# A transformer block with eight experts: the first batch's tokens scattered into slots by expert

## The chip, the cores and the metric

The kernel runs on one core of a Trainium2 chip. A core has a matrix engine (TensorE, PE in the profile, with its weight loads as PEld), VectorE (DVE), ScalarE (ACT), GpSimd (POOL) and a sync engine (SP), each with an instruction queue of its own; semaphores order them. The metric is the device time of one execution in microseconds, lower is better. Before the change it is 930.87 us, the median of three runs (930.03 to 931.92).

## What is computed

One block on x of 2 batches x 1024 tokens x 256 features, in float32. Cut to what matters:

```python
mod = (silu(c) @ wmod).reshape(2, 6, 1, -1)
sa, ca, ga, sb, cb, gb = mod[:, 0], ..., mod[:, 5]
ga = (2 * (ga >= 0) - 1) * maximum(abs(ga), 0.25)       # gb likewise
h = layernorm(x) * (1 + ca) + sa
# 16 query heads of 128 over 4 key heads, sinusoidal positions, causal softmax, projection by wo
x = x + ga * attention(h)
h = layernorm(x) * (1 + cb) + sb
logits = h @ gate_w.T                                   # 8 experts
top_vals, top_idx = top_k(logits, 2)
w = softmax(top_vals)
y_all = einsum('td,eod->teo', h, expert_w) + expert_b   # 256 -> 256 for each expert
x = x + gb * sum(y_all[top_idx] * w)
```

The reference computes all eight experts for every token and picks two; only the two chosen outputs matter.

## The kernel before

Every float32 product is made from a high and a low part of each operand, in three matrix products (high x high, high x low, low x high: `moving_late` L594, `held_late` L602). So each operand is cut on its way: ScalarE writes the high part (`keep_hi`, L1008), VectorE or GpSimd subtracts it for the low part.

The work is two batches of 16 heads ("frames"), then an expert stage. `n` counts the heads of both batches, `l` those of one. Frames 1 to 12 of a batch stand in a loop of three rounds of four, the others are written out. A frame has 12 steps `q` (`STEPS`): in each, TensorE turns a block of probabilities into bank `ps_t` (`turn_probs`, L713), computes a piece of the next head's scores (`ps_s`, L604 to L608), weighs values (`ps_o`, L596 to L600, L723), and, at given steps, the queries of the next head (`queries`, into `ps_m`) and the projection of the previous one by wo (`project`). VectorE masks (L1346), finds the row maximum (L1352), makes low parts of the turned probabilities (`pt_lo`, L1361), brings queries with their bias and position to `raw` (L1378), takes the reciprocal of the row sums (L1390) and adds projections to `acc` (L1399). ScalarE does the exponential (L1058) and the high parts. GpSimd cuts wq and wo of coming heads (L462 to L476) and makes `q_lo` (L483); its order in a frame is q_lo of the next head's second half, cut wq, cut wo, q_lo of the head after it. The sync queue (SP) loads wq and wo head by head (L342, L346).

The scale and shift vectors of the first LayerNorm's modulation and of the second's are computed at the start as columns (`modulate`, L626, 16 products each, read by VectorE); the two gate vectors `ga` and `gb` are needed as rows, and are computed near the end of the heads: one `modulation_rows` (L767) for each batch in heads 14 and 15 of the second batch, from `repeat_silu` and with four VectorE operations (`modulation_part`). In the last head TensorE also turns the expert weights (`turn_weights`), which ScalarE and VectorE cut into `we_hi`, `we_lo`, and the first hidden tile is turned and gated.

The expert stage then runs densely over 16 tiles of 128 tokens, both batches alike. For a tile TensorE does `experts` (four groups, 24 products of 512 columns in all), `turn_coef`, `turn_hidden` (L776) and `gate` (L785) of the next tile, and `mix_bias`. VectorE picks the two best experts (`choose`, from L1589, with the coefficients to L1605), and sums the eight outputs with the token's coefficients (`mix`, eight operations on 128x256), with `statistics` (L1520) and `normalise` of later tiles. GpSimd does `residual` (all of the first batch ahead), `inverse_deviation`, `hidden_lo` and `finish` (three operations, L543 to L550), and SP stores the tile.

The order on every engine is the order of the program; waits stand in front of the instruction that needs them. A wait therefore holds up everything behind it on its engine.

## Time and profile before

| | us |
|---|---|
| Median of three runs | 930.87 (930.03 to 931.92) |
| The profiled execution | 930.91 |
| Span of its trace | 929.1 |
| TensorE busy | 903.3 (97%) |
| VectorE busy | 784.0 (84%) |
| ScalarE busy | 535.6 (58%) |
| GpSimd busy | 274.5 (30%) |

The span reaches from the first to the last recorded instruction; the 1.8 us between it and the execution's time lie outside the trace. A busy share is an average over stages with different limits, so the stages are read one by one, in windows. All times of trace rows are in microseconds from the start of the span, unless they say ns. A row of a timeline or of the chain gives start, length, engine, line and operation, its output and inputs with their shapes and, in brackets, how long the engine had been idle and what released it. "x4" merges four instructions. In the windows "PEclk" is the granted clock of TensorE as a share of 2.4 GHz and "DMA" the mean busy share of the 16 DMA engines. A "q" behind an engine's name (PEldq, SPq) is its queue, which handles registers and DMA issues.

### The profile page before, as it was taken

What the parts mean: (1) busy time and instruction counts of PE and PEld (TensorE: products, weight loads), DVE (VectorE), ACT (ScalarE), POOL (GpSimd) and SP (SyncE); (2) the same over time, 40 slices, a digit from 0 to 9 for tenths busy, and PEclk for the clock granted to TensorE, in tenths of its full rate; (3) what the DMA queues carried; (4) which work ended last, traced back from release to release, by engine and by line L of the source; (5) the groups of instructions that cost most, each with busy time, mean ns of one, the idle gap of its engine ahead of it and who ended that gap; (6) DMA issues with size and microseconds to landing.
All of it is one profiled execution on the core that took longest, in us unless ns stands there. A gap on an engine that the chain in (4) does not pass through costs nothing.

```text
span 929.1 us, 18211 instructions
## 1 busy us (share of the span) xinstructions
PE 903.3 (97%) x5353; PEld 782.5 (84%) x5353; DVE 784.0 (84%) x1775; ACT 535.6 (58%) x1224; POOL 274.5 (30%) x346
## 2 busy tenths in 40 slices
PE   5999999999999999999999999999999999999997
PEld 4688889888898888978888888998888889767775
DVE  5777888888888888888888888888888888899996
ACT  4587666666666666655666666666666655422231
POOL 3454222222222222123322222222222212466544
PEclk9999999999999999999999999999999999999999
DMA  6000000000000000100000000000000022100000
GB/s 215 7 12 13 12 13 12 12 17 17 11 11 11 11 11 7 57 6 1 24 12 12 14 12 11 11 11 11 11 11 11 12 74 92 46 12 17 23 17 24
DMA packets 23764, 21.60 MB, mean 23 GB/s; under 512 B 1530, under 2 KB 22564, under 8 KB 23716
## 3 DMA queue, kind: packets, MB, share of 16 engines
q1 hardware_dynamic: 23652, 20.99, 7.2%
q8 instruction: 24, 0.39, 0.2%
q14 instruction: 24, 0.20, 0.1%
q10 hardware_dynamic: 64, 0.02, 0.0%
HBM read 18.91 MB, written 2.10 MB: 23 GB/s over the span
## 4 chain that ended last, share of the span: by engine, by line
PE 87%; DVE 8%; issue 2%; ACT 1%; DMA 1%; POOL 0%; DVEq 0%; SPq 0%; POOLq 0%; ACTq 0%
PE ps_t L713 13%; PE ps_s L604 9%; PE ps_s L608 9%; PE ps_s L605 9%; PE ps_o L596 7%; PE ps_o L600 7%; PE ps_o L597 6%; PE ps_m L604 3%; PE ps_m L608 3%; PE ps_m L605 3%; PE ps_m L596 3%; PE ps_m L600 3%; PE ps_m L597 3%; PE ps_o L723 1%; DVE acc L1399 1%
## 5 line engine op out<-in xcount | busy, mean ns | idle before, releaser
L1008 ACT ACTIVATE pt_hi<-ps_t 128x512 fp32r<-128x512 f32 (+2 forms) x320 | 170.8, 534 | 142.9 <-PE ps_t L713 142.8
L1058 ACT ACTIVATE probs<-ps_s,neg_max 128x128 f32<-128x128 f32 (+7 forms) x256 | 189.8, 742 | 78.5 <-DVE neg_max L1352 76.5
L1361 DVE TENSOR_TENSOR pt_lo<-ps_t,pt_hi 128x512 fp32r<-128x512 f32 (+2 forms) x320 | 192.3, 601 | 12.7 <-ACT pt_hi L1008 7.6
L1352 DVE TENSOR_REDUCE neg_max<-ps_s 128x1 f32<-128x128 f32 (+7 forms) x256 | 192.6, 752 | 3.7
L713 PE MATMUL ps_t<-ident,probs 128*128 128x128 f32 x1152 | 188.4, 272 | 2.1 <-DVE pt_lo L1361 2.1
L483 POOL TENSOR_TENSOR q_lo<-raw,q_hi 128x512 fp32r<-128x512 f32 x60 | 77.4, 1290 | 358.5 <-ACT q_hi L1008 358.5
L713 PEld LDWEIGHTS ps_t<-ident,probs 128*128 128x128 f32 x1152 | 141.5, 140 | 26.0 <-DVE pt_lo L1361 8.2
L604 PE MATMUL ps_s<-k_hi,q_hi 128*128 128x512 f32 (+2 forms) x354 | 148.6, 420 | 2.3 <-ACT probs L1058 2.3
L1399 DVE SCALAR_TENSOR_TENSOR acc<-ps_m,rsum,acc 128x256 f32<-128x256 f32 x256 | 111.5, 477 | 24.0 <-PE ps_m L608 24.0
L1346 DVE TENSOR_TENSOR ps_s<-ps_s,mask 128x128 f32<-128x128 f32 x256 | 75.7, 296 | 56.6 <-PE ps_s L608 49.8
L608 PE MATMUL ps_s<-k_hi,q_lo 128*128 128x512 f32 (+2 forms) x354 | 123.4, 349 | 0.0
L605 PE MATMUL ps_s<-k_lo,q_hi 128*128 128x512 f32 (+2 forms) x354 | 122.5, 346 | 0.0
L596 PE MATMUL ps_o<-pt_hi,v_hi 128*128 128x512 f32 (+2 forms) x320 | 119.8, 374 | 0.7 <-DVE o_lo L1366 0.7
L600 PE MATMUL ps_o<-pt_lo,v_hi 128*128 128x512 f32 (+2 forms) x320 | 115.6, 361 | 0.0
L597 PE MATMUL ps_o<-pt_hi,v_lo 128*128 128x512 f32 (+2 forms) x320 | 115.1, 360 | 0.0
L604 PEld LDWEIGHTS ps_s<-k_hi,q_hi 128*128 128x128 f32 x354 | 66.9, 189 | 8.0 <-issue 3.2
L604 PE MATMUL ps_m<-wo_hi,o_hi 128*128 128x256 f32 x256 | 72.7, 284 | 0.4 <-DVE acc L1399 0.3
L608 PE MATMUL ps_m<-wo_hi,o_lo 128*128 128x256 f32 x256 | 72.2, 282 | 0.0
L608 PEld LDWEIGHTS ps_s<-k_hi,q_lo 128*128 128x128 f32 x354 | 66.4, 188 | 6.8
L605 PE MATMUL ps_m<-wo_lo,o_hi 128*128 128x256 f32 x256 | 72.1, 282 | 0.0
L605 PEld LDWEIGHTS ps_s<-k_lo,q_hi 128*128 128x128 f32 x354 | 67.6, 191 | 1.9
L600 PEld LDWEIGHTS ps_o<-pt_lo,v_hi 128*128 128x128 f32 x320 | 60.1, 188 | 8.4
(180 smaller groups left out, 1718.3 us busy)
## 6 DMA issues: line engine op xcount, KB each, us to landing
wq_raw<-in_L_attn_wq_dram SPq DMA_DIRECT2D x32, 128.0 KB, 2.2
wo_raw<-in_L_attn_wo_dram SPq DMA_DIRECT2D x32, 128.0 KB, 2.1
wkv_raw<-in_L_attn_wkv_dram SPq DMA_DIRECT2D x2, 1024.0 KB, 6.9
we_raw<-in_L_ffn_expert_w_dram SPq DMA_DIRECT2D x1, 2048.0 KB, 12.1
x_again<-in_L_attn_x_dram SPq DMA_DIRECT2D x2, 1024.0 KB, 10.0
out_dram<-y_out SPq DMA_DIRECT2D x16, 128.0 KB, 1.7
acc<-in_L_attn_x_dram SPq DMA_DIRECT2D x2, 512.0 KB, 4.1
wmod_sb<-in_L_wmod_dram SPq DMA_DIRECT2D x2, 512.0 KB, 8.4
```

The lines of the kernel that those rows point to most:

```text
L596: nc.tensor.matmul(out_ap, a[0], b[0], start=start, stop=False)
L597: nc.tensor.matmul(out_ap, a[1], b[0], start=False, stop=False)
L600: return nc.tensor.matmul(out_ap, a[0], b[1], start=False, stop=stop)
L604: nc.tensor.matmul(out_ap, a[0], b[0], start=start, stop=False)
L605: nc.tensor.matmul(out_ap, a[0], b[1], start=False, stop=False)
L608: return nc.tensor.matmul(out_ap, a[1], b[0], start=False, stop=stop)
L713: last = pe.transpose(ps_t[:, q % 2, col:col + P], probs[par][:, p0:p0 + P], ident[:, :])
L1008: return nc.scalar.activation(dst, src, ACT.Copy, scale=scale)
L1058: nc.scalar.activation(probs[par][:, prob_offset(i):prob_offset(i) + w], ps_s[:, i % 2, col:col + w], ACT.Exp, bias=neg_max[:, par, i:i + ...
L1352: nc.vector.tensor_reduce(neg_max[:, par, i:i + 1], ps_s[:, i % 2, col:col + w], AXIS_X, ALU.max, negate=True).then_inc(max_set, 1)
L1361: nc.vector.tensor_tensor(pt_lo[:, q % PT, lo:CH], ps_t[:, q % 2, lo:CH], pt_hi[:, q % PT, lo:CH].bitcast(F32), ALU.subtract).then_inc(pt_ ...
L1399: last = nc.vector.scalar_tensor_tensor(row, ps_m[:, i * E:(i + 1) * E], rsum[:, par, tile:tile + 1], row, ALU.mult, ALU.add)
```

## The change

The first batch (1024 tokens, eight tiles) no longer goes through the dense stage. The second batch does, as before.

- *Modulation.* All six vectors are now computed as columns at the start: a third `modulate` of 16 products, with `gate_columns` (four VectorE operations) for `ga` and `gb`. GpSimd spreads columns over 128 columns (`spread_columns`), TensorE turns them into rows in side steps, and ScalarE copies them out (`side_read`). `modulation_rows`, `repeat_silu` and `modulation_part` go.
- *The first batch's rows.* During heads 1 to 8 of the second batch GpSimd does the residual and the modulated LayerNorm of one tile a head (`first_residual`, two operations; `hidden_row`, a power and three operations of 128x256), VectorE its statistics (`row_statistics`, three operations). TensorE turns the tile at step 3 and gates it at step 10 of heads 2 to 9 (`side_step`), ScalarE reads both.
- *Placing.* In head 10 VectorE finds each token's two experts and weights and counts them, 33 small operations (`choose_first`); at step 3 of head 12 TensorE ranks tokens with two products (`rank`); in the same head VectorE makes every token's two places and the 23 slots' experts, 15 operations (`place_rows`).
- *Scattering.* In heads 13 and 14 GpSimd writes the rows to `slot_rows_dram` by eight indirect DMAs each, between wo's cut and the next q_lo. Each expert's tokens fill whole slots of 128 rows; 23 slots hold any distribution (2048 choices / 128 + 7). The buffer is filled with x before, so that rows that no token takes are finite.
- *The slot stage* stands ahead of the dense one: SP loads 20 + 3 slots after the last scatter and the last head's scores; each is turned, cut and multiplied by the one expert of the slot (six products of 256 columns), which TensorE picks by a register; VectorE adds the bias row of that expert, by a register as well, and SP stores the slot to `slot_out_dram`. Turn and gate of the second batch's first four tiles stand between the slots.
- *Collecting.* In the dense stage, now eight tiles, GpSimd gathers each first-batch token's two output rows by indirect DMA (two for each tile, four in each of the first four steps), ScalarE weighs one, VectorE weighs the other, adds, applies the gate and adds the residual (`join`, three operations), and SP stores.
- The second batch's heads are written out in full in place of the loop, since their work now differs from head to head.

The core of the diff:

```diff
+SLOTS = 2 * T // P + EXPERTS - 1
+SLOT_PLANES = 3
+SLOT_OUT = 3
+HELD_SLOTS = 20
+AHEAD = 4
...
+SIDE = ([("rows", 0, q, v) for q, v in ((2, 0), (3, 1), (10, 2), (11, 3))]
+        + [u for i in range(NT) for u in (("turn", 2 + i, 3, i), ("gate", 2 + i, 10, i))]
+        + [("rank", 12, 3, 0)]
+        + [("rows", HEADS - 1, q, v) for q, v in ((2, 0), (3, 1))])
+SIDE_AT = {(l, q): (s, kind, i) for s, (kind, l, q, i) in enumerate(SIDE)}
...
+            sp.wait_ge(scattered, 16 * FREE * NT)
+            sp.dma_start(x_again[1][:, :, :], x_tiles[:, NT:2 * NT, :]).then_inc(x_again_in[1], 16)
+            sp.wait_ge(t_mm, NS * (B * HEADS - 1))
+            sp.wait_ge(s_mm, NT * B * HEADS)
+            sp.wait_ge(q_lo_set, NC * B * HEADS)
+            slot_v = slot_dram.rearrange("(s p) e -> p s e", p=P)
+            half = HELD_SLOTS // 2
+            sp.dma_start(slot_rows[:, 0:half, :], slot_v[:, 0:half, :]).then_inc(slots_in[0], 16)
+            sp.dma_start(slot_rows[:, half:HELD_SLOTS, :], slot_v[:, half:HELD_SLOTS, :]).then_inc(slots_in[1], 16)
+            sp.dma_start(slot_rows_more[:, :, :], slot_v[:, HELD_SLOTS:SLOTS, :]).then_inc(slots_in[2], 16)
+            sp.dma_start(ebias_all[:, :, :].rearrange("p x o -> p (x o)"),
+                         expert_b.rearrange("x o -> (x o)").partition_broadcast(P)).then_inc(ebias_in, 16)
...
+                sp.wait_ge(slot_out, s + 1)
+                sp.dma_start(y_dram[s * P:(s + 1) * P, :], y_slot[:, s % SLOT_OUT, :]).then_inc(y_stored[s % SLOT_OUT], 16)
...
+            def scatter_rows(i):
+                if i == 0:
+                    pool.wait_ge(place_set, 1)
+                    pool.wait_ge(row_set, NT)
+                    pool.wait_ge(slots_filled, 32)
+                for f in range(FREE):
+                    pool.indirect_dma_start(
+                        slot_dram, bass.IndirectOffsetOnAxis(ap=r_place_u[:, f, i:i + 1], axis=0),
+                        x_rows[:, i, :], None).then_inc(scattered, 16)
...
+            def gather(i):
+                if i == 0:
+                    for j in range(SLOT_OUT):
+                        pool.wait_ge(y_stored[j], 16 * len(range(j, SLOTS, SLOT_OUT)))
+                for f in range(FREE):
+                    pool.indirect_dma_start(
+                        picked[:, f, i, :], None, y_dram,
...
+            for m in range(NT):
+                for i in (2 * m, 2 * m + 1):
+                    if i < NT:
+                        gather(i)
+                if m + 6 < NT:
+                    normalise(m + 6)
+                if m > 0:
+                    finish(m - 1)
+                if m + 2 < NT:
...
-            def modulation_rows(b, bank):
-                pe.wait_ge(silu_b_set, 1)
-                pe.wait_ge(gmod_in, 48)
-                for m in range(2):
+            def side_step(l, q):
+                s, kind, i = SIDE_AT[l, q]
+                spare = ps_t[:, q % 2, :]
+                if kind == "rows":
+                    spread = spread0 if l == 0 else spread1
+                    pe.wait_ge(spread_set, KE * (i + 1) + (0 if l == 0 else 4 * KE))
                     for k in range(KE):
+                        last = pe.transpose(spare[:, k * P:(k + 1) * P], spread[:, i * KE + k, :], ident[:, :])
+                elif kind == "turn":
+                    pe.wait_ge(row_set, i + 1)
+                    for k in range(KE):
+                        last = pe.transpose(spare[:, k * P:(k + 1) * P], x_rows[:, i, k * P:(k + 1) * P], ident[:, :])
+                elif kind == "gate":
+                    pe.wait_ge(side_set, side_count("turn", i))
+                    for k in range(KE):
+                        last = pe.matmul(spare[:, 0:EXPERTS], row_t[:, k, :], gate_t[:, k, :],
...
+            def slot_product(s, e):
+                if s == 0:
+                    pe.wait_ge(we_lo_set, EXPERTS // 2 * KE)
+                if s >= 2:
+                    pe.wait_ge(slot_out, s - 1)
+                pe.wait_ge(slot_hi_set, s + 1)
+                for k in range(KE):
+                    w = [t[:, k, bass.ds(e, 1), :].rearrange("p x o -> p (x o)") for t in (we_hi, we_lo)]
+                    i = s % SLOT_PLANES
+                    last = held_late(kv_bank(2 + s % 2)[:, 0:O], (slot_hi[i][:, k, :], slot_lo[i][:, k, :]), w,
+                                     k == 0, k == KE - 1, (slot_lo_set, s + 1) if k == 0 else None)
+                last.then_inc(slot_mm, 1)
...
+            _, slot_e = nc.values_load_multi_w_load_instructions(
+                slot_expert_u[0:1, 0:SLOTS], engines=[mybir.EngineType.PE], min_val=0, max_val=EXPERTS - 1,
+                skip_runtime_bounds_check_because="a sum of seven comparisons lies in 0 to 7")
+            for s in range(SLOTS):
+                if s + 2 < SLOTS:
+                    turn_slot(s + 2)
+                slot_product(s, slot_e[s])
...
+            def choose_first(q):
...
+                    nc.vector.tensor_tensor(r_weight[:, 1, :], r_egap[:, :], r_weight[:, 0, :], ALU.mult)
+                    nc.vector.memset(r_before[:, 0, :], 0.0)
+                    nc.vector.tensor_copy(r_before[:, 1, :], r_both[:, 0, :]).then_inc(r_dve, 1)
+                    for i in range(1, NT):
+                        dve.wait_ge(r_dve, done + 6 + i)
+                        nc.vector.tensor_tensor(r_before[:, i + 1, :], r_before[:, i, :], r_both[:, i, :],
+                                                ALU.add).then_inc(*((r_dve, 1) if i + 1 < NT else (r_count_set, 1)))
...
+            def slot_finish(s, e):
+                dve.wait_ge(slot_mm, s + 1)
+                if s == 0:
+                    dve.wait_ge(ebias_in, 32)
+                if s >= SLOT_OUT:
+                    dve.wait_ge(y_stored[s % SLOT_OUT], 16 * (s // SLOT_OUT))
+                nc.vector.tensor_tensor(y_slot[:, s % SLOT_OUT, :], kv_bank(2 + s % 2)[:, 0:O],
+                                        ebias_all[:, bass.ds(e, 1), :].rearrange("p x o -> p (x o)"),
+                                        ALU.add).then_inc(slot_out, 1)
...
+            def join(i):
+                par = i % 2
+                dve.wait_ge(first_part_set, i + 1)
+                nc.vector.scalar_tensor_tensor(both_parts[:, par, :], picked[:, 1, i, :], r_weight[:, 1, i:i + 1],
+                                               first_part[:, par, :], ALU.mult, ALU.add).then_inc(join_step, 1)
+                dve.wait_ge(join_step, 2 * i + 1)
+                nc.vector.tensor_tensor(both_parts[:, par, :], both_parts[:, par, :], mod_rows0[:, 1, :],
+                                        ALU.mult).then_inc(join_step, 1)
+                if i >= 2:
+                    dve.wait_ge(joined_done[par], 16 * (i // 2))
+                dve.wait_ge(join_step, 2 * i + 2)
+                nc.vector.tensor_tensor(joined[:, par, :], both_parts[:, par, :], acc[:, i, :],
+                                        ALU.add).then_inc(joined_set, 1)
```

## Rows read from the trace of the kernel before

**Rows 1.** Windows: length, busy us: PE, PEld, DVE, ACT, POOL; PEclk, DMA, GB/s.
```profile
0.00:23.00 23.00, 13.18 (x51) 11.31 (x52) 13.65 (x43) 10.37 (x17) 8.85 (x18) 1.00 0.62 218
474.00:770.00 296.00, 295.04 (x1865) 264.37 (x1864) 254.53 (x532) 186.40 (x422) 61.65 (x76) 1.00 0.07 21
804.30:923.50 119.20, 116.58 (x536) 86.63 (x534) 106.14 (x364) 34.71 (x109) 62.32 (x91) 1.00 0.05 17
891.60:912.90 21.30, 21.30 (x101) 16.15 (x100) 18.56 (x64) 6.65 (x22) 9.70 (x14) 1.00 0.06 20
923.50:929.10 5.60, 0.00 (x0) 0.00 (x0) 0.87 (x2) 0.00 (x0) 2.17 (x3) 0.80 0.07 23
```

**Rows 2.** Waits of the looped heads, 474 to 770: us, times, longest.
```profile
PEld ps_t L713 <- DVE pt_lo L1361: 2.6, 13, 0.2
```

**Rows 3.** Timeline, VectorE: one rsum reciprocal ends each head.
```profile
570.92 0.17 DVE L1390 RECIPROCAL rsum<-sums 128x4 f32<-128x4 f32 x1
...
593.30 0.17 DVE L1390 RECIPROCAL rsum<-sums 128x4 f32<-128x4 f32 x1
...
749.90 0.17 DVE L1390 RECIPROCAL rsum<-sums 128x4 f32<-128x4 f32 x1
...
773.64 0.17 DVE L1390 RECIPROCAL rsum<-sums 128x4 f32<-128x4 f32 x1
```

**Rows 4.** Chain of waits: start, length, engine, work.
```profile
776.64 1.73 PE ps_m L767 x8
...
808.78 0.12 PE ps_m L605
...
809.38 0.23 PE ps_t L776 x2
...
885.15 0.54 PE ps_o L785 x4
...
886.72 0.23 PE ps_s L605
```

**Rows 5.** Line 998, a register instruction on TensorE's queue (least/median/largest ns).
```profile
L998 PEldq FUSED_REGOPS  x3: 50/55/55, 811.6 to 871.3; - x3
```

**Rows 6.** Timeline, VectorE: a pt_lo of 128x256.
```profile
575.01 0.39 DVE L1361 TENSOR_TENSOR pt_lo<-ps_t,pt_hi 128x256 fp32r<-128x256 f32 x1
```

**Rows 7.** Groups by line and form, 790 to 929: busy us, mean ns, idle.
```profile
L1520 DVE BATCH_NORM_STATS2 st<-acc 128x6 f32 x12 | 5.0, 418 | 0.0
...
L1605 DVE TENSOR_TENSOR wtop<-egap,wtop 128x1 f32<-128x1 f32 x16 | 4.2, 260 | 0.5
```

**Rows 8.** Timeline: a VectorE CAST alone, then one beside GpSimd's finish.
```profile
866.51 0.17 DVE L1599 CAST top_f<-top_i 128x2 f32<-128x2 uint32 x1
...
887.11 0.75 POOL L550 TENSOR_TENSOR y_out<-y_sum,acc 128x256 f32<-128x256 f32 x1 [0.28 <-POOL y_sum L547]
887.12 0.76 DVE L1599 CAST top_f<-top_i 128x2 f32<-128x2 uint32 x1
```

**Rows 9.** Line 342, issues of the sync queue (ns).
```profile
L342 SPq DMA_DIRECT2D wq_raw<-in_L_attn_wq_dram x30: 368/373/1283, 60.6 to 726.5; - x30
```

**Rows 10.** Page, section 6: DMA issues.
```profile
wq_raw<-in_L_attn_wq_dram SPq DMA_DIRECT2D x32, 128.0 KB, 2.2
...
we_raw<-in_L_ffn_expert_w_dram SPq DMA_DIRECT2D x1, 2048.0 KB, 12.1
```

**Rows 11.** Timeline: one head's first turns, and GpSimd's wo_hi and q_lo.
```profile
555.69 0.60 PE L713 MATMUL ps_t<-ident,probs 128*128 128x128 f32 x4
...
567.84 0.40 POOL L473 TENSOR_SCALAR wo_hi<-wo_raw 128x256 fp32r<-128x256 f32 x1 [4.83 <-PE ps_m L608]
...
577.93 1.28 POOL L483 TENSOR_TENSOR q_lo<-raw,q_hi 128x512 fp32r<-128x512 f32 x1 [8.87 <-ACT q_hi L1008]
```

**Rows 12.** Timeline, TensorE at the start: a modulation, a wait for raw.
```profile
28.43 1.95 PE L626 MATMUL ps_m<-silu_c,wmod_sb 128*128 128x2 f32 x16 [0.15 <-DVE v_bias L1552]
...
44.08 0.50 PE L604 MATMUL ps_t<-wv_hi,h_hi 128*128 128x512 f32 x1 [1.30 <-DVE raw L1322]
```

966 lines of the change are left out of this document (601 added, 365 removed).

## The prediction

> **What bounds the kernel now.** I read the table of windows first: in the looped heads of batch 1 TensorE is busy 295.0 of 296 us [rows 1]. The list of waits says that this is a true bound: over the same stretch its only repeated wait is for pt_lo, 2.6 us in 13 pieces [rows 2]. One head takes 22.38 us, from one rsum reciprocal to the same of the next head [rows 3]. So whatever the change puts on TensorE inside the heads comes out in full; VectorE has 14% of each head free, some 3.1 us (254.5 of 296 us busy [rows 1]), ScalarE and GpSimd much more. Then the windows: the dense expert stage runs from 804.3 to 923.5, 119.2 us for 16 token tiles [rows 1], 7.45 us a tile. From 891.6 to 912.9 TensorE is busy all of 21.3 us for three tiles, 7.1 us each [rows 1]; the chain of waits gives 0.23 us for a 512-column product and 0.12 for a 256-column one [rows 4], so 24 products of 512 columns are 5.5 us of a tile. The last 5.6 us are GpSimd's finish and the store, with the clock falling only there [rows 1].
>
> **What the change takes away: half of the dense stage.** Batch 0's eight tiles (24 products of 512 columns each) go, and 23 slots come, each with two transposes (0.23) and six products of 256 columns (6 x 0.12): 0.95 us of TensorE [rows 4], 21.9 in all against 8 x 5.5 = 44. That is the core gain, 22 us; the slots are counted for the worst case, so the columns fall to 1 part in 2.8 and not to a quarter. In the slot stage stand also what batch 1 needs ahead: four turns (0.23) and gates (0.54), 3.1 us, and two projections, 1.4. A slot's weights are picked by a register: per product perhaps one register instruction, which costs 0.050 to 0.055 us on TensorE's queue [rows 5], 6 a slot; hidden they cost nothing, bare 7 us over the stage.
> VectorE in the slot stage: two 128x256 operations a slot (0.39 each [rows 6]), 18 us, six statistics at 0.9 (0.42 and two short ones [rows 7]), four best-two choices at 0.7, three coefficient chains at 1.1 to 2.2 and four accumulations (1.7): 32 us. Both engines near 30 us, with two-deep banks between them, so they don't overlap fully: bounds 28 us (TensorE alone, with 1.6 us of first latency) and 42 (bare register work, and half of VectorE's 13 us of extra pieces uncovered). I take 37, nearer the upper, since each slot's transposes wait for the VectorE operation two slots back. Batch 1's dense tiles: four at 7.1, then four without turn and gate (0.23 + 0.54 [rows 4]) at 6.33, 53.7; the second tile is VectorE's (mix 3.3, eight at 0.39 and what lies between, statistics 0.9, choice and coefficients 2.3, the new join's three operations 1.3: 7.8), another 0.9. With 0.5 between the stages: 37 + 0.5 + 54.6 = 92.1.
>
> **GpSimd in the dense stage.** It now issues two indexed gathers for each of eight tiles, four in each of the first four steps, ahead of its old work there (finish 3 x 0.73 [rows 8], hidden_lo 0.73, normalise 1.0). No row shows a transfer issued by GpSimd. Bounds for one issue, g: 0.37 us, which an issue on the sync queue holds its queue for [rows 9], and 2.1, as if GpSimd were held until a 128 KB transfer lands (2.2 from issue to landing [rows 10]). I take 1.5, nearer the upper, because 128 row numbers are read and turned into addresses by program, and a 128x256 pass of GpSimd alone is 0.73. GpSimd begins about 3 us late (the last slot store must be issued and land, about 2.2). Step 0: 3 + 4g + 1.7 = 10.7; step 1: + 4g + 1.0 + 0.73 = 18.5 until tile 0's sum is out, which tile 2's mix waits for at 15.5 us: 3 late; steps 2 and 3 are each 4g + 2.9 = 8.9 against 7.1: 1.8 and 1.9 late. Sum 7 us; at g = 1.0 it is nothing, at 2.1 it is 16.
> The Trainium skill, DMA: Bandwidth & Descriptors, Specifications, gives a first byte after about 1 us for a GpSimd transfer and 0.6 for a sync one; taken as g = 1.0 this would strike the 7 us. No run here shows either.
>
> **What it adds in the heads.** TensorE, all at full price: 12 turns at 0.23 (four of the modulation rows, eight of hidden rows), eight gates at 0.54, one ranking product of two fp32 pieces at about 0.6 (bounds 0.24, two at a 256-column product's 0.12, and 1.7, a modulation product's group): 7.7 us [rows 4]. VectorE: row_statistics, 0.9 in eight heads, is under the 3.1 us of slack, nothing (4 us if it weren't). Head 10's choice is 33 small operations at about 0.22 (260 ns is the mean of such a one [rows 7], 0.17 the least [rows 8]), 7.3 us in one head that has 3.1 free, a third of which lies after the work: 3.5 us late, bounds 0 (spread over the next head) and 6. Head 12's placing, 15 at 0.26, 3.9: 1.0 late. GpSimd: residual and hidden row, 4.2 us a head, lie in its long waits (8.87 us before one q_lo [rows 11]); nothing. Its scatters, eight in head 13 and eight in head 14, stand behind wo's cut and in front of the next q_lo. The cut starts 12.15 us into the head and ends at 13.4; the scatters take 8g = 12, q_lo 1.3: ready at 26.7, wanted by the next head's second score piece, 3.2 us into it, at 25.6 (the head begins at its first turns, 555.69 [rows 11]): 1.1 us. The unrolled second batch adds fetches but no wait that I can see: heads 13 and 14 of batch 0, outside its loop, take the same 22.4.
> Start: a third modulation, 16 products in 1.95 us [rows 12], and gate_columns, four VectorE operations (1.0 at 0.26 each), lie ahead of the first queries, with some 0.9 from engine to engine between them. TensorE is 3.9 late, and it later gives back the waits for raw (1.3 us in one piece [rows 12], some 0.5 in smaller ones): 2.0 (bounds 1 and 4). The spread columns lie in GpSimd's idle head; nothing.
>
> **Heads 14 and 15.** The two products for modulation rows go: head 14 was 23.74 against 22.38 [rows 3], so 1.4 back. In head 15 go the 1.73 us product [rows 4], one turn and gate (0.8), and VectorE loses some 8 us of modulation and statistics, with which 2 us of TensorE's waits go; two row turns and two slot turns come (0.9): 3.6 back.
> But the sync queue waits for all scatters before it loads the slots: they end 13.4 + 8g = 25.4 into head 14 and land 2 later, 5 us into head 15. Then 4.9 MB follow (x 1.0, slots 2.9, the bias rows 1.0). we_raw's 2 MB landed in 12.1 with about 1.5 MB beside it [rows 10], some 270 GB/s: 18 us, so the bias rows, last in line, land about 24 us into head 15. TensorE is through at 19.6, then both engines load 23 expert numbers into registers (unseen; 23 times 0.05, a register instruction, or 0.26, a small VectorE operation: 1 to 6 us, I take 2), and slot 0's finish wants the bias at 22.9. Registers and bias together: 4 us (bounds 1 and 14).
>
> **The sum.** Start 2.0, TensorE in heads 7.7, choice and placing 4.5, q_lo 1.1, heads 14 and 15 -5.0, registers and loads 4.0, expert stages 92.1 + 7 - 119.1 = -20.0: together -5.7 against the span of 929.1. 923.4, and with the 1.8 us that lie outside it in the profiled execution (930.9, which is the median too) 925.2 us.
>
> **Rivals.** (A) *GpSimd keeps up.* With g at 1.0 or less the 7 us and the 1.1 go, 2 of the loads' 4, and with cheap registers the slots take 32: 925.2 - 15.1 = 910. For it: GpSimd is idle 48% of the dense stage now [rows 1].
> (B) *Slower: GpSimd becomes the bound*, at scatters and gathers both. It decides from g of about 1.7: by the same steps the dense stage then loses 9.8 in place of 7, q_lo and the slot loads 1.6 more each, 6.0 together, and the gain is gone. At 2.1: 9 + 4.8 + 4.8, and 3 in the slots, 947. For it: an operation on VectorE that took 0.17 alone takes 0.76 beside GpSimd's pass [rows 8], so these two hold each other up, and the dense stage has both busy. The Trainium skill, SBUF — State Buffer, A bandwidth-pool intuition that's wrong, tells of a GpSimd transfer of 0.62 us that took 3.1 beside a VectorE copy, since its descriptors couldn't be written; a g of 3.1 would by the steps above give some 980, an estimate. Nothing here shows it, and most VectorE operations in these stages read PSUM.
> (C) *The clock falls in the slot stage*, where small products stand between waits: if a third of its 27 us of TensorE work ran at 1.2 GHz, +8: 933. Against: in the first 23 us TensorE is busy 57% and is granted 2.4 GHz; lower levels appear only after its last product [rows 1].
> That the change doesn't do what it says I give nothing: fixed counts make the work the same whatever the routing.
>
> **Chances.** The sum 45% (its own range 917 to 934: faster 0.33, same 0.05, slower 0.07), A 26%, B 23%, C 6% (slower, but for 0.01). Within 0.2% (1.9 us, about what a measurement can tell) 0.07; faster 0.59; slower 0.34. The low end takes the slots at 32 us, no wait for GpSimd and a choice half hidden (905); the high end is B with little more (949).
>
> **What would show it.** TensorE's heads 2 to 9 of batch 1 at 23.1 us, head 10 near 26; in head 13 a wait for q_lo; the scatters' and gathers' own spans on GpSimd near 1.5; slot stage 37, dense stage 61 to 62 with mixes waiting for y_sum; ebias as the last releaser of slot 0. Wrong it would be if an indexed issue is far from 1.5, if register-addressed products take longer than 0.12 by more than 0.05, or if the long VectorE heads are absorbed.

## The result

The changed kernel takes 915.37 us, the median of four runs (914.43 to 916.02), against 931.28 of the kernel before (the median of four as well); the ratio is 0.983, its 95% interval 0.9813 to 0.9847. Its profiled execution has a span of 913.8 us, 15.3 less than before. The forecast was 925.2 in a range of 905 to 949: the right side, and the time inside the range, but a gain of 6 us where 16 were measured. The step that failed is the sum of the stages behind the heads: it had the slots at 37.5 us with the piece between the stages, where the trace has 32.7, and GpSimd's gathers at 7 us on top of the dense stage, where it has 2.6.

Busy time on the page of the profile after (before: TensorE 903.3, VectorE 784.0, GpSimd 274.5):

```profile
PE 877.7 (96%) x5337; PEld 768.4 (84%) x5337; DVE 758.9 (83%) x1725; ACT 531.9 (58%) x1223; POOL 320.9 (35%) x395
```

The windows of the changed kernel, to be read against [rows 1] (length, busy time of PE, PEld, DVE, ACT, POOL, then clock, DMA share, GB/s). They are a stretch of the second batch's heads, TensorE's wait ahead of the slots, the slot stage, the dense stage and the tail:

```profile
470.00:760.00 290.00, 289.41 (x1849) 259.72 (x1848) 255.89 (x591) 182.06 (x427) 102.90 (x133) 1.00 0.04 13
814.75:816.15 1.40, 0.01 (x2) 0.03 (x1) 0.66 (x2) 0.60 (x1) 0.00 (x0) 1.00 0.02 6
816.15:848.86 32.71, 29.20 (x216) 25.58 (x217) 27.14 (x100) 12.80 (x38) 20.62 (x26) 1.00 0.25 82
848.86:906.10 57.24, 55.62 (x242) 39.91 (x240) 47.08 (x142) 14.99 (x47) 39.97 (x47) 1.00 0.23 71
906.10:913.80 7.70, 0.13 (x1) 0.00 (x0) 4.57 (x8) 0.00 (x0) 2.40 (x3) 0.85 0.21 69
```

TensorE is still busy all through the heads (289.4 of 290 us). The slot stage is 32.7 us, the dense stage of eight tiles 57.2 with 55.6 of TensorE, and the tail 7.7 against 5.6 before. The heads' lengths, from one rsum reciprocal to the next as in [rows 3] (the second of each head; the first pair spans head 3, the last three rows heads 14 and 15):

```profile
511.60 0.17 DVE L1674 RECIPROCAL rsum<-sums 128x4 f32<-128x4 f32 x1
...
534.53 0.17 DVE L1674 RECIPROCAL rsum<-sums 128x4 f32<-128x4 f32 x1
...
763.75 0.17 DVE L1674 RECIPROCAL rsum<-sums 128x4 f32<-128x4 f32 x1
...
787.79 0.17 DVE L1674 RECIPROCAL rsum<-sums 128x4 f32<-128x4 f32 x1
...
811.76 0.17 DVE L1674 RECIPROCAL rsum<-sums 128x4 f32<-128x4 f32 x1
```

A head that holds a turn and a gate takes 22.93 us against 22.38, head 14 is 24.04 and head 15 23.97. Put together against the trace before, in us:

| | forecast | measured |
|---|---|---|
| start, to the last head of batch 0 | +2.0 | +3.2 |
| turns, gates, rows and ranking on TensorE | +7.7 | +4.7, ranking in the next row |
| choice, ranking and placing (heads 10 to 13) | +4.5 | +1.9 |
| what goes from heads 14 and 15 | -5.0 | -6.0 |
| scatters' harm to heads 14 and 15 | +1.1 | +5.8 |
| between the heads and slot 1's products | +4.0 | +2.1 |
| slots | 37 + 0.5 | 32.7 |
| dense stage | 54.6 + 7 | 57.2 |
| tail | 5.6 | 7.7 |

TensorE is through with the heads 10.45 us later than before (814.75 against 804.3; the first five rows give 9.6, and 0.8 of the sixth lies ahead of that moment), and the expert stages with the tail are 99.05 us against 124.8: together -15.3. The row of heads 14 and 15 is split with the first experiment, which has them without scatters: 22.40 and 19.79, against 23.74 and 24.41 before. So the forecast had the moment at which the heads end nearly right (+10.3), by errors that cancel, which is luck, and the whole miss of 9.6 us lies behind it.

The row of the start holds something that isn't work. In this profiled execution the granted clock fell for a while at the start, which it didn't before the change. The same stretch in the changed kernel and in the paced run below, whose start is the same:

```profile
24.00:40.00 16.00, 14.08 (x68) 11.05 (x67) 9.77 (x30) 8.44 (x17) 7.67 (x7) 0.89 0.04 10
...
24.00:40.00 16.00, 14.27 (x77) 11.43 (x76) 10.90 (x31) 8.50 (x18) 7.30 (x7) 1.00 0.03 10
```

From the second modulation to TensorE's first wait for a row of probabilities it is 36.8 us in the first and 35.2 in the second (27.69 to 62.89): the lower clock cost 1.6 us, and it comes in some executions and not in others.

What harmed heads 14 and 15 is seen in the timeline of ScalarE and TensorE (the bracket gives the idle time before and what ended it), and in two windows:

```profile
769.56 0.60 ACT L1233 ACTIVATE pt_hi<-ps_t 128x512 fp32r<-128x512 f32 x1 [2.89 <-remote]
...
771.40 0.35 PE L787 MATMUL ps_s<-k_hi,q_hi 128*128 128x256 f32 x1 [1.39 <-ACT probs L1283]
...
793.39 0.60 ACT L1233 ACTIVATE pt_hi<-ps_t 128x512 fp32r<-128x512 f32 x1 [4.22 <-remote]
...
794.77 0.44 PE L954 MATMUL ps_t<-ident,spread 128*128 128x128 f32 x2 [3.70 <-DVE pt_lo L1645]
...
790.00:794.00 4.00, 1.07 (x10) 0.83 (x8) 1.38 (x2) 0.61 (x2) 3.07 (x6) 1.00 0.27 98
794.00:800.00 6.00, 5.23 (x27) 4.77 (x28) 3.44 (x7) 3.54 (x9) 0.00 (x0) 0.72 0.88 280
```

ScalarE stood 2.9 us ahead of head 14's first pt_hi and 4.2 ahead of head 15's, "remote" being a releaser that the profile can't name; both came free 1.4 us after the end of the last scatter of a row of eight. TensorE lost 1.4 and 3.7 us. After the second its granted clock fell to the lower of its two levels for a while: 0.72 is the mean of 794 to 800, a mixture of 1.2 and 2.4 GHz. The scatters themselves (shortest, median and longest ns):

```profile
L642 POOL DMA_INDIRECT slot_rows_dram<-x_again,r_place_u x16: 956/960/1263, 758.0 to 791.0; - x16
```

0.96 us each, and 0.30 between two: g is 1.26 us.

### The profile page after: what moved, and what is told of

Same layout as the page of the kernel before. It is cut to its first block, busy times and chain, and to the rows that moved or that the text cites. A ratio compares the mean times of both kernels' runs of the same rounds, so it can differ in the third digit from the quotient of the medians.

```text
span 913.8 us, 16758 instructions
## 1 busy us (share of the span) xinstructions
PE 877.7 (96%) x5337; PEld 768.4 (84%) x5337; DVE 758.9 (83%) x1725; ACT 531.9 (58%) x1223; POOL 320.9 (35%) x395
## 4 chain that ended last, share of the span: by engine, by line
PE 84%; DVE 7%; POOL 2%; issue 2%; ACT 2%; DMA 1%; another core or an unknown queue 0%; SPq 0%; DVEq 0%; ACTq 0%; POOLq 0%
PE ps_t L898 13%; PE ps_s L787 8%; PE ps_s L791 8%; PE ps_s L788 8%; PE ps_o L783 7%; PE ps_o L779 7%; PE ps_o L780 7%; PE ps_m L787 3%; PE ps_m L791 3%; PE ps_m L788 3%; PE ps_m L779 3%; PE ps_m L783 3%; PE ps_m L780 3%; PE ps_o L908 1%; POOL picked L737 1%
```

## Experiments

All times that follow are medians, with the ratio to the kernel before on the same chip; the changed kernel itself stands at 0.983.

### No scatters

```diff
-                    pool.indirect_dma_start(
-                        slot_dram, bass.IndirectOffsetOnAxis(ap=r_place_u[:, f, i:i + 1], axis=0),
-                        x_rows[:, i, :], None).then_inc(scattered, 16)
+                    pool.sem_inc(scattered, 16)
```

> Leaves the 16 scatters out (the slots then hold rows of x, so the output isn't the reference's); GpSimd raises the semaphore itself, so everything that waits for them goes on. Theory 1: the scatters' transfers are what ScalarE waits for at the starts of heads 14 and 15 (2.9 and 4.2 us, TensorE 1.4 and 3.7 us behind it, then 1.6 us lost at 1.2 GHz). Then all of it goes, head 14 comes to about 22.5 us and head 15 to 20, and the kernel takes about 908.5. Rival: those waits belong to the heads written out in full, whose instructions have to be fetched, and stay without scatters: then no more than 1 us is gained, 914.5.

909.28 us, ratio 0.9769 (0.9747 to 0.9791). ScalarE isn't held, TensorE doesn't wait, and the reciprocals of heads 14 and 15 (that of head 13 was at 763.12) show heads of 22.40 and 19.79 us:

```profile
785.52 0.17 DVE L1672 RECIPROCAL rsum<-sums 128x4 f32<-128x4 f32 x1
...
805.31 0.17 DVE L1672 RECIPROCAL rsum<-sums 128x4 f32<-128x4 f32 x1
```

Theory 1 holds: 5.8 us of the two heads are the scatters' doing, and the heads' code being written out isn't enough for it: it is as long here, but for the 16 scatters.

### Plain transfers in place of the scatters

```diff
-                    pool.indirect_dma_start(
-                        slot_dram, bass.IndirectOffsetOnAxis(ap=r_place_u[:, f, i:i + 1], axis=0),
-                        x_rows[:, i, :], None).then_inc(scattered, 16)
+                    pool.dma_start(slot_dram[(f * NT + i) * P:(f * NT + i + 1) * P, :],
+                                   x_rows[:, i, :]).then_inc(scattered, 16)
```

> Each scatter is replaced, at its place, by a plain GpSimd transfer of the same 128 rows to fixed places (the rows are then not sorted by expert, so the output isn't the reference's). Theory A: it is the indexed form that holds ScalarE (TensorE waits 1.4 and 3.7 us); then both waits vanish, heads 14 and 15 take 22.4 and 19.8, about 909. Theory B: any GpSimd transfer at that place does it; then the waits stay, 915. An issue is expected at 0.4 to 1.3 us.

911.37 us, ratio 0.9792 (0.9776 to 0.9808). Heads 14 and 15 take 22.40 and 19.79 again: theory A, it is the indexed form. The issues of that line (shortest, median and longest ns):

```profile
L642 POOL DMA_DIRECT2D slot_rows_dram<-x_again x16: 542/542/808, 759.6 to 785.7; - x16
```

0.54 us for a plain transfer of 128 KB on GpSimd, against 1.26 for an indexed one.

### The scatters elsewhere in their heads, in groups of four, and paced

```diff
+                if b == 1 and l == SCATTER_FRAMES[1]:
+                    for i in range(4, NT):
+                        scatter_rows(i)
                 if nxt2:
                     cut_wq(n + 2, par)
+                if b == 1 and l == SCATTER_FRAMES[0]:
+                    scatter_rows(0)
+                    scatter_rows(1)
```

(Tiles 2 and 3 stay behind wo's cut in head 13.)

> The same 16 scatters, earlier in their heads: in head 13 four after wq's cut and four after wo's, in head 14 all eight right after the first q_lo, so that none is under way when a head ends. Theory: ScalarE is held only where scatters fall on the few instructions at a head's end (766 to 769 and 789 to 793 us); moved away, heads 14 and 15 take 22.4 and 19.8 as without scatters, 909.5. Rival 1: ScalarE is held wherever eight scatters run, the waits only move: 915. Rival 2: GpSimd's late wo cut (by some 4 us in head 14) becomes a wait of TensorE: 912.

912.66 us, ratio 0.9817 (0.9801 to 0.9833). Behind head 13's two groups of four nobody waits long. In head 14 the eight in a row, now from 771.5 to 781.3, hold ScalarE there:

```profile
777.22 0.60 ACT L1238 ACTIVATE o_hi<-ps_o 128x512 fp32r<-128x512 f32 x1 [1.88 <-remote]
778.66 0.60 ACT L1238 ACTIVATE pt_hi<-ps_t 128x512 fp32r<-128x512 f32 x1 [0.84 <-remote]
...
782.26 0.88 DVE L1688 SCALAR_TENSOR_TENSOR acc<-ps_m,rsum,acc 128x256 f32<-128x256 f32 x2 [2.28 <-remote]
...
783.06 1.09 ACT L1238 ACTIVATE pt_hi<-ps_t 128x512 fp32r<-128x512 f32 x2 [2.86 <-remote]
```

Head 14 takes 26.22 us and head 15 18.91. So ScalarE is held at either place of the row of eight, which is rival 1 for head 14, and it isn't held alone: VectorE, too, stood 2.3 us without a releaser that the profile can name. The groups of four left head 13 at 21.46 us, against 21.40 in the changed kernel.

From that kernel, the row of eight is split in two:

```diff
                 if b == 1 and l == SCATTER_FRAMES[1]:
-                    for i in range(4, NT):
-                        scatter_rows(i)
+                    scatter_rows(4)
+                    scatter_rows(5)
...
-                if b == 1 and l == SCATTER_FRAMES[0]:
-                    scatter_rows(2)
-                    scatter_rows(3)
+                if b == 1 and l in SCATTER_FRAMES:
+                    k = 2 + 4 * SCATTER_FRAMES.index(l)
+                    scatter_rows(k)
+                    scatter_rows(k + 1)
```

> The 16 scatters in four groups of four: in head 13 after wq's and after wo's cut, in head 14 after the first q_lo and after wo's cut. In the run with head 13's groups of four and head 14's eight together, ScalarE was held in head 14 only. Theory: a row of eight is what holds it, four are taken without a wait: head 14 about 22.5, head 15 at most 20.5, ratio to the kernel before 0.977 (909.5). Rival: it is head 14's code or place, not the number: then waits of 2 to 4 us stay in head 14 or 15, 0.981 or more.

909.94 us, ratio 0.9771 (0.9755 to 0.9788). Heads 14 and 15 take 22.39 and 19.77, as without scatters, and in head 15 the clock stays at full speed:

```profile
785.70:805.50 19.80, 18.54 (x134) 16.70 (x133) 16.06 (x32) 12.54 (x27) 1.62 (x4) 1.00 0.78 261
...
828.00:832.00 4.00, 4.00 (x21) 3.79 (x21) 2.75 (x12) 1.40 (x5) 2.78 (x4) 0.57 0.29 98
```

The second row lies in this run's slot stage, where the clock did fall, for about 3.5 us.

The third run of this kind leaves head 14's eight together, and spaces them:

```diff
+                    if slow:
+                        for _ in range(2):
+                            pool.tensor_scalar(every[:, :], ident[:, :], 0.0, 1.0, ALU.mult, ALU.add).then_inc(pace, 1)
...
```

> As the run with the scatters early, but each of head 14's eight is followed by two short GpSimd operations of about 0.35 us, so that they are issued every 2 us in place of 1.26 (they then end some 6 us later, wo's cut with them). Theory: ScalarE is held because eight scatters issued back to back pile up; paced they don't, and its waits in head 14 (1.9, 0.8 and 2.9 us) vanish. Rival: they are held as before, once or more, at any pace.

908.6 us (two runs only), ratio 0.9758 (0.9738 to 0.9777). ScalarE isn't held at all; head 14 takes 22.35 and head 15 20.39, in which TensorE waits 1.8 us for the spread gate columns, since GpSimd makes them behind the last scatter. That wait made the head 0.6 us longer than without it. Whether it is the pacing that helps isn't shown, as the next run tells.

### The third modulation left out, and code shifted

```diff
                             pe.wait_ge(rows_set, 1)
-                            modulate(2)
+                            pe.wait_ge(wmod_in[2], 32)
...
-                            gate_columns()
+                            dve.wait_ge(wmod_in[2], 32)
+                            nc.vector.memset(modt[:, MOD_GA:MOD_GB + 1, :, :], 0.5).then_inc(modt_set, 1)
```

> Leaves out the third modulation's 16 products and the four operations of gate_columns at the start (the gates are a constant, so the output isn't the reference's); their weights are still loaded and waited for. The prediction gave the start 2.0 us (bounds 1 and 4): ratio 0.981. Rival: it is the load of these weights ahead of the others, or the later start of the run that each profile shows differently, and nothing comes back: 0.983.

908.38 us, ratio 0.9756 (0.974 to 0.9773): 7 us less, more than either theory. Two rows of TensorE show where. The first, TensorE's first wait for a row of probabilities, measures the start; the second is its wait in head 15:

```profile
62.26 0.36 PE L787 MATMUL ps_s<-k_hi,q_hi 128*128 128x256 f32 x1 [0.61 <-ACT probs L1283]
...
789.09 0.41 PE L954 MATMUL ps_t<-ident,spread 128*128 128x128 f32 x2 [1.83 <-POOL spread L597]
```

The same row of the changed kernel, with the second modulation from which both are counted:

```profile
27.99 1.17 PE L809 MATMUL ps_m<-silu_c,wmod_sb 128*128 128x2 f32 x9 [0.45 <-DVE v_bias L1908]
...
64.77 0.36 PE L787 MATMUL ps_s<-k_hi,q_hi 128*128 128x256 f32 x1 [0.61 <-ACT probs L1283]
```

From the second modulation to that wait it is 36.8 us in the changed kernel (27.99 to 64.77), 34.6 here (27.68 to 62.26), both with the clock at 0.89 in 24 to 40, and 33.3 before at full clock: the third modulation costs 2.2 us, or 1.9 by the traces with a full clock (35.2 against 33.3). The other 5 us are the scatters' stalls, which are gone although the scatters stand as before in rows of eight: head 14 takes 22.41, head 15 20.44 with the 1.8 us wait for the spread columns. The gates being constant, the tokens' experts are others here; but with constant places (below) the stalls stay, so the places alone don't explain it. What else differs is that TensorE's and VectorE's code is shorter ahead of the heads.

The chip differs as well. The runs in groups of four, paced, without the third modulation and the first combined one below were taken on one chip, and none of their traces has a stall, this one in spite of its rows of eight. All other experiments were run on two other chips, and there every trace with a row of eight back to back has one (for the changed kernel itself the chip isn't on record). So it may be the chip and not the edit that spared this run; nobody ran the changed kernel's rows on that chip unedited. For the paced run this leaves nothing shown. That groups of four help stands also on the other chips: in head 13 above, and in the last run below.

Two runs, on a chip where the stalls came, shift the code and leave the work alone:

```diff
+            for _ in range(96):
+                pe.sem_inc(spare_pe, 1)
             modulate(0)
```

> The changed kernel with 96 semaphore increments on TensorE's queue at the start, where TensorE waits 6 us for its first weights; all else is as it was, so TensorE's code lies 96 instructions further on and its loads of code during heads 13 and 14 (one a head, in the rows of the instruction queue at 765 and 785 us) come at other moments. Theory: ScalarE is held when a load of code falls into a long row of scatters; then its waits of 2.9 and 4.2 us shrink or vanish, ratio to the kernel before about 0.976. Rival: TensorE's code has nothing to do with it: waits as before, 0.983.

```diff
+            for _ in range(96):
+                act.sem_inc(spare_act, 1)
             cut_weights(0, 0)
```

> The same on ScalarE's queue (96 semaphore increments before its first cut of weights, where it waits). Theory: if it is ScalarE's own code that comes late behind the scatters, ScalarE's waits move or vanish, ratio 0.976 to 0.980. If it is TensorE's, they stay as they were, 0.983.

With TensorE's code shifted 923.05 us, ratio 0.9918 (0.9902 to 0.9935): the increments took longer than the 6 us that they were to hide in, and the heads start some 8 us later, which is the whole loss. With ScalarE's shifted 914.62, ratio 0.9843 (0.9819 to 0.9868). The first of them: its stall in head 14, then in head 15 the last scatter, ScalarE's first pt_hi and TensorE's wait, and last the wait that the increments became:

```profile
777.50 0.60 ACT L1236 ACTIVATE pt_hi<-ps_t 128x512 fp32r<-128x512 f32 x1 [2.86 <-remote]
...
799.00 0.96 POOL L643 DMA_INDIRECT slot_rows_dram<-x_again,r_place_u  x1 [0.31 <-issue]
...
799.96 0.60 ACT L1236 ACTIVATE pt_hi<-ps_t 128x512 fp32r<-128x512 f32 x1 [2.85 <-PE ps_t L901]
...
801.33 0.44 PE L957 MATMUL ps_t<-ident,spread 128*128 128x128 f32 x2 [2.34 <-POOL spread L598]
...
18.53 0.77 PE L810 MATMUL ps_s<-silu_c,wmod_sb 128*128 128x2 f32 x3 [15.72 <-issue]
```

The same pt_hi of head 15 in the run with ScalarE's code shifted, and in the one without the third modulation, where nothing holds it:

```profile
792.81 0.60 ACT L1234 ACTIVATE pt_hi<-ps_t 128x512 fp32r<-128x512 f32 x1 [2.85 <-issue]
...
786.39 0.60 ACT L1233 ACTIVATE pt_hi<-ps_t 128x512 fp32r<-128x512 f32 x1 [1.03 <-PE ps_t L898]
```

In both shifted runs ScalarE is still held 2.9 us at head 14. At head 15 it stands 2.85 us, where 1.0 is the wait without a stall and 4.2 that of the changed kernel: the stall is there, but shorter, and ends with the last scatter (799.96; in the other run 792.75 and 792.81) and not 1.4 us behind it. TensorE waits 2.3 us, for this and for the spread columns at once. The two heads take 22.56 and 21.47 us; after nearly the same wait the granted clock fell in the first (0.92 on the mean of the head) and stayed at full speed in the second. So the theory that TensorE's loads of code decide fell: shifting either engine's code left one stall of two as it was and shortened the other. What is shown: where a stall of over 1 us came, a long row of indexed transfers was under way, and its length hangs on something that shifted code changes. What that is, and whether the chip has a part in it, stays open.

### Gathers

```diff
-                for i in (2 * m, 2 * m + 1):
-                    if i < NT:
-                        gather(i)
+                gather(m)
```

> GpSimd gathers one tile's rows in each of the eight steps of the dense stage, in place of two tiles' in each of the first four; nothing else. Theory: GpSimd's four issues of 1.26 us a step put it 2.6 us behind, which TensorE pays in tiles 4 and 5; with two a step (2.5 us) it keeps up, the dense stage falls from 57.2 to 54.6 and the kernel to 912.8. Rival: the waits of tiles 4 and 5 come from ScalarE's own order of work, and nothing changes: 915.4.

913.51 us, ratio 0.9805 (0.9788 to 0.9822). In the changed kernel TensorE's tiles 0 to 7 follow each other by 7.14, 7.11, 7.11, 7.18, 7.99, 7.64 and 6.57 us; with one tile's gathers a step by 7.13, 7.11, 7.11, 7.79, 6.62, 7.19 and 6.53, which is 1.3 us less in sum (the medians differ by 1.9). TensorE's waits for other engines in tiles 4 and 5 of the changed kernel, and VectorE's wait for GpSimd's sum in its dense stage (total, times, longest):

```profile
885.39 0.47 PE L787 MATMUL ps_s<-we_hi,h_hi 128*128 128x512 f32 x1 [0.56 <-ACT h_hi L1233]
...
893.03 0.47 PE L787 MATMUL ps_s<-we_hi,h_hi 128*128 128x512 f32 x1 [0.67 <-DVE y_odd L1999]
...
DVE y_even L1997 <- POOL y_sum L747: 2.3, 2, 1.6
```

The wait for h_hi and those for y_sum are gone with one tile's gathers a step; what is left are two waits of TensorE of 0.5 us, for ScalarE's coef_t and VectorE's mix. So the chain of the forecast, mixes that wait for y_sum, is there, and the theory holds with half the sum worked out: 1.3 us for 2.6. The other 1.3 us above 54.6 don't come from four gathers a step; no run takes the gathers away altogether.

```diff
+                pool.indirect_dma_start(
+                    slot_rows[:, i, :], None, y_dram,
+                    bass.IndirectOffsetOnAxis(ap=r_place_u[:, 0, i:i + 1], axis=0)).then_inc(gathered[i], 16)
```

> A third gather for each tile, into a buffer that nobody reads: six issues in each of the first four steps in place of four. Theory (the prediction's own steps with g at the measured 1.26): step 0 ends at 3 + 7.6 + 1.7 = 12.3, step 1 at 21.6 against 15.5, then twice 10.5 against 7.1: 12.8 us late in place of 2.8, so 10 us more, 925.4. Rival: GpSimd has slack elsewhere in the stage and the issues are hidden: at most 3 us more, 918.

924.33 us, ratio 0.9924 (0.9908 to 0.9941): 8.8 us more by the ratios and 9.8 in the dense stage of the traces, against 10 worked out. Tiles 2 to 4 take 11.0, 10.7 and 10.4 us. Two waits of the dense stage:

```profile
DVE y_even L2000 <- POOL y_sum L750: 5.1, 1, 5.1
...
PE ps_s L790 <- DVE y_odd L2002: 8.7, 3, 3.7
```

VectorE's mix waits for GpSimd's y_sum 5.1 us, and TensorE behind it: this is the chain that the forecast described, at its full size only with six gathers a step.

### Registers

```diff
-            pe.wait_ge(place_set, 1)
-            _, slot_e = nc.values_load_multi_w_load_instructions(
...
+            slot_e = [s % EXPERTS for s in range(SLOTS)]
```

> The slots' experts are fixed numbers (slot mod 8) in place of registers, and the register loads of TensorE and VectorE go (wrong experts, so the output isn't the reference's). The prediction's steps: 2 us for loading registers and up to 6 for their use in the slot stage; by the trace after, TensorE's 1.39 us wait at the stage's start holds the loading. Theory: 1.4 us at most, 914.0. Rival: register instructions are a part of the slot stage's 32.7 us (about 0.05 for each of 138 products): 7 us less, 908.

916.16 us, ratio 0.9849 (0.9833 to 0.9866), no faster. In the trace TensorE's idle time at the stage's start goes from 1.40 to 0.16 us, and from the first slot's turn to the dense stage it is 34.6 us against 35.9:

```profile
817.03 0.38 PE L791 MATMUL ps_m<-wo_hi,o_lo 128*128 128x256 f32 x1 [0.16 <-DVE o_lo L1647]
...
787.30:812.60 25.30, 21.03 (x134) 19.10 (x133) 16.17 (x32) 12.65 (x27) 5.72 (x10) 0.87 0.67 225
...
832.00:840.00 8.00, 6.63 (x42) 6.50 (x43) 7.19 (x31) 3.29 (x10) 4.72 (x7) 0.79 0.27 89
```

That is 1.3 us, nearly all at the stage's start; products whose weights are picked by a register follow each other by the same 0.12 us as the others. It isn't sharp: the clock fell in this run's slot stage (the last row) and not in the changed kernel's, and the same stage with registers took from 35.5 to 37.0 us in the traces of the other runs. The 7 us of the rival are ruled out. In the profiled execution the gain is lost again in head 15, which took 25.27 us here; its clock was 0.87 against 0.93 in the same head of the changed kernel. How long the clock stays low after the stall differs between these two.

### Choice and placing

```diff
-                    if b == 1 and l == CHOOSE_FRAME:
-                        choose_first(q)
-                    if b == 1 and l == RANK_FRAME:
-                        place_rows(q)
+                    if b == 1 and l == RANK_FRAME and q == 10:
+                        nc.vector.memset(r_weight[:, :, :], 0.5)
```

> Leaves out the choice in head 10, the ranking product and the placing in head 12 (places and weights are constants, so the output isn't the reference's). The prediction had 3.5 + 1.0 us for VectorE and 0.6 for the ranking: 5.1 less, 910.3. By heads 10 to 13 of the trace after (23.47, 22.74, 23.75, 21.40, sum 91.36 against four times 22.38 = 89.52) it is 1.8: 913.6.

913.13 us, ratio 0.9823 (0.9806 to 0.9839). Heads 10 to 13 take 22.80, 22.42, 22.40 and 22.40 in place of 23.47, 22.74, 23.75 and 21.40: 1.3 us, where the forecast had 5.1 with the ranking. In the changed kernel many of the 48 operations of VectorE follow each other after 0.07 to 0.25 us, which is the likely reason that they cost so little.

### The tail

```diff
-                if m > 0:
-                    join(m - 1)
-            join(NT - 1)
+                for i in JOINS.get(m, ()):
+                    join(i)
...
+JOINS = {1: (0,), 2: (1,), 3: (2,), 4: (3,), 5: (4, 5), 6: (6, 7)}
```

> The joins of the first batch's tiles 4 to 7 (three VectorE operations each, with ScalarE's weighing) go after tiles 5 and 6 of the dense stage, in place of one after each tile and two after the last. Theory: the tail of 7.7 us against 5.6 before is the two joins behind the last mix; with none there GpSimd's finish ends last again: 2.1 us less, 913.3. Rival: VectorE bounds tiles 5 and 6 once they hold two joins (3.9 + 2 x 1.3 us against 6.4 of TensorE), so the time comes back there: 915 or more.

916.64 us, ratio 0.9839 (0.9823 to 0.9855). The changed kernel's tail, for comparison: the last joins on VectorE, and GpSimd's last finish that runs beside them.

```profile
907.57 0.83 DVE L2010 TENSOR_TENSOR both_parts<-both_parts,mod_rows 128x256 f32<-128x256 f32 x1
...
908.50 0.76 DVE L2015 TENSOR_TENSOR joined<-both_parts,acc 128x256 f32<-128x256 f32 x1
...
909.19 0.94 DVE L2007 SCALAR_TENSOR_TENSOR both_parts<-picked,r_weight,first_part 128x256 f32<-128x256 f32 x1
...
910.69 0.43 DVE L2015 TENSOR_TENSOR joined<-both_parts,acc 128x256 f32<-128x256 f32 x1
...
909.06 0.78 POOL L751 TENSOR_TENSOR y_out<-y_sum,acc 128x256 f32<-128x256 f32 x1
```

The joins end at 911.1, GpSimd's finish at 909.8. Moved ahead, they make VectorE late for the last mixes, so that GpSimd's last finish begins 2.9 us behind the end of TensorE's last product (908.1), not 1.1 (907.3 behind 906.2):

```profile
910.93 0.72 POOL L748 TENSOR_TENSOR y_sum<-y_even,y_odd 128x256 f32<-128x256 f32 x1 [4.88 <-DVE y_odd L1999]
```

The rival holds. Beside GpSimd the join's operations take 0.76 to 0.94 us, alone 0.43 to 0.48. The last two runs put parts of the joins on GpSimd and have the scatters in groups of four and the gathers spread as well. The joins' part of the first:

```diff
+                if m + 1 == NT:
+                    weigh_second(NT - 2)
+                    weigh_second(NT - 1)
                 mix(m, range(4, EXPERTS))
...
+            for i in (NT - 2, NT - 1):
+                pool.tensor_tensor(both_parts[:, par, :], both_parts[:, par, :], mod_rows0[:, 1, :],
+                                   ALU.mult).then_inc(pool_joined, 1)
```

> Three edits together: the scatters in groups of four; one tile's gathers in each dense step but the fourth, which has two; and the gate and residual of the last two joins on GpSimd ahead of its last finish, where it waits 3.9 us, their weighing on VectorE ahead of the last four mixes. If the effects add: 6 us from the scatters, 1.9 from the gathers (as measured), 2 from the tail: about 905.5, ratio 0.972. Rival: the gain of the tail is eaten by VectorE as when the joins went early: 907.5 or more.

910.09 us, ratio 0.9775 (0.9758 to 0.9791), no better than the groups of four alone: GpSimd, busy with two joins, begins its last finish at 902.1, 1.4 us after the last mix, and with the two gathers more in step 3 tiles 4 and 5 take 6.95 and 7.86, against 6.62 and 7.19 with one tile's gathers a step.

The last run, shown against the one before it, keeps one of them there, and the last join on VectorE:

```diff
                 if m + 1 == NT:
-                    weigh_second(NT - 2)
-                    weigh_second(NT - 1)
+                    weigh_second(NT - 2)
...
-                for i in GATHERS.get(m, ()):
-                    gather(i)
+                gather(m)
```

> Scatters in groups of four, one tile's gathers a step, and of the joins only the last but one ends on GpSimd, so that GpSimd is free when the last mix ends and VectorE does the last join beside its finish. Effects added: 6 us (scatters), 1.7 (gathers), 1.5 to 2 (tail): about 905.7, ratio 0.973. Rival: the tail doesn't shrink, 907.5, ratio 0.975.

907.83 us (905.79 to 907.93), ratio 0.9759 (0.9742 to 0.9775), with one join on GpSimd and one tile's gathers a step. Its dense stage and tail:

```profile
841.30:897.30 56.00, 54.96 (x242) 40.17 (x240) 49.88 (x143) 15.02 (x47) 40.91 (x48) 1.00 0.24 73
897.30:904.00 6.70, 0.18 (x1) 0.00 (x0) 2.84 (x6) 0.00 (x0) 3.21 (x5) 0.81 0.24 81
```

The tail is 6.7 us, one less than 7.7, and the dense stage 56.0. By the ratios this is 6.6 us under the changed kernel, 5.5 of them from the scatters; to the groups of four alone the gain isn't clear of the intervals. The profiled execution is the fastest of the four, and the clock didn't fall in it before the last product. Heads 14 and 15 take 22.61 and 19.77 us: on a chip on which rows of eight were held, groups of four weren't, but for waits of ScalarE and VectorE below 1 us.

## Why the prediction was right or wrong

The forecast of a gain of 5.7 us failed at the stages behind the heads. Its steps "I take 37, nearer the upper" for the slots and "I take 1.5, nearer the upper" for one indexed issue were each too near the upper of two bounds that hold: the slots took 4.8 us less, and the gathers 4.4 less. Registers and loads were too dear by 1.9, and the tail, which had no term, took 2.1 back. In the heads errors of 5 us and more cancel. Term by term:

- *The core gain*, 22 us of TensorE by counting columns: right. The slot stage has 29.2 us of TensorE in 32.7.
- *Slots at 37*: the choice between the bounds of 28 and 42 was wrong. The argument was that TensorE and VectorE, both near 30 us with two banks between them, would not overlap well; they do (TensorE is idle 3.5 us, the longest pieces 0.8). Too dear by 4.8 with the 0.5 between the stages.
- *GpSimd's gathers*: the chain of waits was there, its term g mis-sized, 1.5 for 1.26. By the forecast's own steps g = 1.26 gives 2.8 us in place of 7, and the dense stage is 57.2 where 54.6 + 2.8 = 57.4 would be expected. That the two agree is in part luck: with one tile's gathers a step only 1.3 of the 2.6 us went. With six gathers a step the steps give 10 us more, and 8.8 to 9.8 were measured. So the truth lies between the sum and rival A, and rival B's point, g of 1.7, wasn't reached. The Trainium skill, DMA: Bandwidth & Descriptors, Specifications, would have struck these us with g = 1.0, an estimate; 1.26 lies halfway between it and my 1.5, and the gathers still cost what remains. Its other place, SBUF — State Buffer, A bandwidth-pool intuition that's wrong, wasn't met: no issue beside VectorE held GpSimd for over 1.26 us, against the 3.1 that it tells of.
- *The scatters*: the forecast looked for q_lo behind them (1.1 us) and found nothing else. Head 13's q_lo began late, at 768.2, but TensorE never waited for it, and head 14 has none behind its scatters; by the forecast's own steps g = 1.26 makes it ready at 24.8, ahead of the 25.6 at which it is wanted. What cost 5.8 us was ScalarE, held during a long row of indexed transfers, with the lower clock behind it. Nothing in the trace before shows that. GpSimd's spread columns, which stand behind the scatters and are wanted at step 2 of head 15, could have been read from the diff: where no stall covers it, that wait is 1.8 us and makes the head 0.6 longer. The step failed there by not listing every thing that is queued behind the scatters. Rival B's reason, that GpSimd and VectorE hold each other up, shows in the tail (0.43 alone, 0.76 to 0.94 beside GpSimd). In the heads VectorE, too, stood for up to 2.3 us with the scatters early, but behind what isn't known.
- *TensorE's side work at full price*: right in kind, too dear in size. A turn and a gate were put at 0.23 + 0.54; the heads grew by 0.55. The gate's 0.54 of [rows 4] contains a latency that the next work covers: the changed kernel's gate at 826.27 is followed by the next transposes 0.36 later. With the four row turns it is 4.7 for 7.1, too dear by 2.4.
- *Choice and placing*: 4.5 + 0.6 against 1.3 to 1.9. The mean of 260 ns in [rows 7] is a duration; issued in a row, such operations can follow each other faster. The term was mis-sized, the direction right. Its 3.5 us for head 10 don't follow from its own numbers either: 7.3 us in a head with 3.1 free are 4.2 late, before anything is said of where the free time lies.
- *Registers and loads*: 4.0 against about 2.1, of which 1.3 are the registers, as the static run shows. The bias rows weren't the last releaser of slot 0.
- *Start*: 2.0 against 3.2. The third modulation itself is 1.9 to 2.2, so the term was right; the rest is the clock, which fell at the start of the profiled execution (1.6 us) and which no step of the forecast had.
- *The tail* had no term at all. Two joins stand behind VectorE's last mix. They take 4.1 us (907.06 to 911.12), since GpSimd's finish runs beside them, and end 1.3 behind it; the tail is 2.1 longer.
- *Rival C*: in the changed kernel's trace the clock didn't fall in the slot stage (1.00). It fell in head 15, after a stall that the forecast hadn't. In the traces of five other runs it did fall in the slot stage, for some 3.5 us (0.57 over four in the row with groups of four), and the stage, leaving out the static run, took 36.0 to 36.8 us against 35.5 to 37.0 in those where it didn't: far from rival C's 8 us, but not its zero either.

## What to carry to other kernels

Cost small operations and short matmul groups by the distance at which they follow each other, not by their durations; here that alone made the heads 4 to 5 us too dear, which the total hid, since the scatters' stalls cost as much. Ahead of a row of slow issues, list everything behind it on its queue, and then who waits for that: the cheapest repair of this change was to split 16 indexed transfers into groups of four in the queue's gaps, which brought 5.5 us. Look at the granted clock of every stretch before pricing it: at the start it made 1.6 of 3.2 us. And a stage's end deserves a term of its own: work that fits between others in the middle stands bare behind the last one.
